# Attention of a decoder layer: products of raw x with the rms scale applied behind them, one scan per head, the first layer norm folded into the second, no transposes of h

## The reference

```
h      = x * rsqrt(mean(x*x) + 1e-6) * norm_w
q,k,v  = h Wq, h Wk, h Wv       (8 heads of 64); rope on q and k
f,g,o  = sigmoid(h Wbeta + b), sigmoid(h Wig + b), sigmoid(h Wog + b)   (one per head and token)
M_t    = M_{t-1} * f_t + g_t / 8 * k_t v_t^T ;  y_t = o_t * q_t M_t
x1     = layernorm(x + y Wout + bout)                 # first layer norm
r_t    = 0.9 r_{t-1} + ctx_t * ctx_t
x2     = layernorm(x1 + x1 * r)                       # second layer norm
out    = layernorm(x2 + FFN(x2)),  FFN: 8 experts, 512 -> 2048 -> 512, with its own norm in front
```

## Time and profile before

| | us |
|---|---|
| median of 3 runs | 1409.67 |
| lowest and highest of the runs | 1406.32, 1410.07 |
| the profiled execution, its own time | 1414.41 |
| span of the profiled execution | 1412.6 |
| PE busy in the span | 1332.6 (94%) |
| DVE busy | 816.3 (58%) |
| POOL busy | 637.2 (45%) |
| ACT busy | 470.9 (33%) |

### The profile page before, as it was taken

One profiled execution on the slowest core, in us unless ns is written; L12 is line 12 of the kernel. 1 busy time (PEld: TensorE's weight loads), 2 busy tenths in 40 slices (PEclk: granted clock), 3 DMA queues, 4 the chain that ended last, 5 costly groups with the idle time before them and its releaser, 6 DMA issues.

```text
span 1412.6 us, 17999 instructions
## 1 busy us (share of the span) xinstructions
PE 1332.6 (94%) x6458; PEld 1051.4 (74%) x6458; DVE 816.3 (58%) x1464; ACT 470.9 (33%) x675; POOL 637.2 (45%) x357
## 2 busy tenths in 40 slices
...
GB/s 227 60 60 76 60 48 57 74 74 74 60 74 60 30 74 74 60 46 112 75 231 60 63 200 44 212 94 48 200 60 197 108 32 214 60 178 128 21 129 30
DMA packets 63990, 133.66 MB, mean 95 GB/s; under 512 B 4800, under 2 KB 5440, under 8 KB 61888
## 3 DMA queue, kind: packets, MB, share of 16 engines
...
## 4 chain that ended last, share of the span: by engine, by line
PE 74%; DVE 18%; issue 5%; ACT 1%; DMA 1%; DVEq 0%; SPq 0%; POOL 0%; POOLq 0%; ACTq 0%
PE qk_ps L84 6%; PE qk_ps L86 6%; PE qk_ps L85 6%; PE v_ps L84 5%; PE v_ps L85 5%; PE v_ps L86 5%; DVE decays L855 4%; PE gate_ps L84 4%; PE gate_ps L86 4%; PE gate_ps L85 4%; PE y_ps L84 4%; DVE decays L854 4%; PE y_ps L85 3%; PE y_ps L86 3%; PE s_ps L84 3%
## 5 line engine op out<-in xcount | busy, mean ns | idle before, releaser
L695 POOL TENSOR_TENSOR rot<-rot 128x1024 f32<-128x1024 f32 x32 | 81.8, 2557 | 254.1 <-DVE rot L880 254.1
L1025 DVE CAST yT_hi<-gate_ps 128x512 fp32r<-128x512 f32 x62 | 42.9, 692 | 180.8 <-ACT gate_ps L630 180.8
L1025 DVE CAST yT_hi<-v_ps 128x512 fp32r<-128x512 f32 x62 | 42.9, 691 | 172.4 <-ACT v_ps L630 172.4
L84 PE MATMUL qk_ps<-wqkv_hi,hT 128*128 128x512 f32 x256 | 103.6, 405 | 2.4 <-DVE wqkv_lo L807 2.4
L630 ACT ACTIVATE gate_ps<-gate_ps,b_cols 128x512 f32<-128x512 f32 x64 | 42.2, 660 | 190.1 <-PE gate_ps L86 190.1
L85 PE MATMUL qk_ps<-wqkv_lo,hT 128*128 128x512 f32 x256 | 100.0, 391 | 0.0
L86 PE MATMUL qk_ps<-wqkv_hi,hT 128*128 128x512 f32 x256 | 99.6, 389 | 0.0
L769 POOL TENSOR_TENSOR wqkv_lo<-h_squares,wqkv_hi 128x2048 fp32r<-128x2048 f32 x15 | 69.3, 4623 | 66.9 <-ACT wqkv_hi L597 66.9
L733 POOL TENSOR_TENSOR rstd_b<-mean_var_b,ln_eps_b 128x4 f32<-128x4 f32 x15 | 3.0, 202 | 211.4 <-DVE mean_var_b L1013 211.4
L630 ACT ACTIVATE v_ps<-v_ps,b_cols 128x512 f32<-128x512 f32 x64 | 42.3, 661 | 157.2 <-PE v_ps L86 156.3
L855 DVE TENSOR_TENSOR_SCAN decays<-f_all,diag 128x128 f32<-128x128 f32 x128 | 89.0, 695 | 0.0
(11 more groups left out here) (267 smaller groups left out, 3784.3 us busy)
## 6 DMA issues: line engine op xcount, KB each, us to landing
...
```

The costliest lines, as they stand in the source:

```text
L84: eng.matmul(out, lhs_hi, rhs_hi, start=first, stop=False)
L695: pool.tensor_tensor(a, a, rot_b[j], ALU.add).then_inc(rot_done, 1)
L1025: dve.tensor_copy(high, up_ps[c % 2][:]).then_inc(hid_hi_done, 1)
```

## The change

The rms scale depends on the token alone, so it can be applied behind the products. The changed kernel therefore:

- loads x a second time, already transposed (`xT`, an input laid out by the host), and splits it on ACT (`x_high`) and POOL (`x_low`). `scale_h`, `turn_h`, `h_high` and `h_low` are gone, and with them 8 transposes on PE;
- puts the rms scale into the rope tables (`scale_rope` on ACT), into the gate of v (`token_gates`) and, for the gates, into a product with `rms_rows`, which reach all rows through a small round trip to DRAM (`spread_rms`);
- makes one scan of 384 elements per head of the two of 256 and 128, with a zero between the parts (`clear_f`), two DMAs for the two parts of `f_all`, one buffer of decays in place of two, and another order of scans;
- leaves the first layer norm out as a pass: `add_memory` subtracts its mean on the way, and since the second norm divides by its own deviation, the first deviation enters only through its epsilon (`norm_scale`, six small POOL instructions in place of two times two). The second normalisation moves from DVE to ACT (`scale_x2`);
- orders the bodies anew on PE, DVE, ACT and POOL.

The core of the diff (left out: allocation, waits renamed from h to xT, and where the expert stage's buffers lie):

```diff
-SCANS = {3: (0,), 4: (1, 2), 5: (3, 4, 5), 6: (6, 7)}
+SCANS = {3: (0, 1), 5: (2, 3, 4, 5), 7: (6, 7)}
...
+            def load_xT(b):
+
+                if b.n >= 1:
+                    sp.wait_ge(xT_lo_done, (b - 1).after(1, 1))
+                sp.dma_start(xT_raw[:], xT[b.index].rearrange("(k p) t -> p k t", p=P)).then_inc(xT_in, 16)
...
+            def spread_rms(b):
+
+                sp.wait_ge(rms_done, b.after(1, 1))
+                for j in range(NT):
+                    sp.dma_start(rms_dram[b.odd, j * P:(j + 1) * P].rearrange("(p a) -> p a", a=1), rms[:, b.odd, j:j + 1])\
+                        .then_inc(rms_stored, 16)
+                sp.wait_ge(rms_stored, b.after(32, 32))
+                sp.dma_start(rms_rows[:], rms_dram[b.odd].partition_broadcast(NG)).then_inc(rms_in, 16)
...
+                rows = f_dram[b.odd].rearrange("(h t) -> h t", h=NH)
+                sp.dma_start(f_all[:, :, P:DW], rows.partition_broadcast(P)).then_inc(f_in, 16)
+                sp.dma_start(f_all[:, :, 0:P], rows[:, P:L].partition_broadcast(P)).then_inc(f_in, 16)
...
+                if (b + 1).within(B):
+                    spread_rms(b + 1)
                 if (b + 2).within(B):
                     load_x(b + 2)
+                    load_xT(b + 2)
...
+            def x_high(b):
+
...
+                act.activation(xT_hi[b.odd], xT_raw[:], ACT.Copy).then_inc(xT_hi_done, 1)
+
+            def scale_rope(b):
...
+                for j in range(NT):
+                    act.activation(rope_x[:, j, :], rope_sb[:, j, :], ACT.Copy,
+                                   scale=rms[:, b.odd, j:j + 1]).then_inc(rope_scaled, 1)
...
+            def scale_x2(b):
+
+                act.wait_ge(shift_done, b.after(1, 1))
+                for j in range(NT):
+                    act.activation(res[:, j, :], res[:, j, :], ACT.Identity, bias=shift[:, j:j + 1],
+                                   scale=rstd[:, j:j + 1]).then_inc(x2_done, 1)
...
+                    if (b - 2).within(B) and b.n <= B and c == 0:
+                        scale_x2(b - 2)
...
                 if (b + 1).within(B):
-                    h_high(b + 1)
...
+                if b.n >= 0 and (b + 1).within(B):
+                    scale_rope(b + 1)
...
+                    if e.i is None and e.n == 0 and c == 1:
+                        scale_x2(Step(B - 1))
...
+            def x_low(b):
+                pool.wait_ge(xT_hi_done, b.after(1, 1))
+                pool.tensor_tensor(xT_lo[b.odd], xT_raw[:], xT_hi[b.odd].bitcast(F32), ALU.subtract).then_inc(xT_lo_done, 1)
...
+            def norm_scale(b):
+
+                pool.wait_ge(mean_done[1], b.after(NT, NT))
...
+                    pool.wait_ge(x2_done, (b - 1).after(NT, NT))
+                pool.tensor_tensor(shift[:], mean_var[0][:, :, 1], ln_eps[:], ALU.add).then_inc(eps_scaled, 1)
+                pool.wait_ge(eps_scaled, b.after(2, 1))
+                pool.tensor_tensor(shift[:], shift[:], ln_eps[:], ALU.mult).then_inc(eps_scaled, 1)
+                pool.wait_ge(eps_scaled, b.after(2, 2))
+                pool.tensor_tensor(rstd[:], mean_var[1][:, :, 1], shift[:], ALU.add).then_inc(var_eps, 1)
+                pool.wait_ge(var_eps, b.after(1, 1))
+                pool.tensor_tensor(rstd[:], rstd[:], minus_half[:], ALU.pow).then_inc(rstd_done, 1)
+                pool.tensor_tensor(shift[:], mean_var[1][:, :, 0], minus_one[:, 0:NT], ALU.mult).then_inc(minus_mean, 1)
+                pool.wait_ge(rstd_done, b.after(1, 1))
+                pool.wait_ge(minus_mean, b.after(1, 1))
+                pool.tensor_tensor(shift[:], shift[:], rstd[:], ALU.mult).then_inc(shift_done, 1)
...
+                    if b.n == -1:
+                        x_low(b + 1)
                     rms_scale(b + 1)
+                    if b.n >= 0:
+                        x_low(b + 1)
                 if (b - 2).within(B):
-                    norm_scale(b - 2, 1)
+                    norm_scale(b - 2)
                 if (b - 1).within(B):
                     context_low(b - 1)
                 if b.n == B:
                     split_w2(Step(0), 0)
                 if b.within(B):
                     rotate(b, 0)
+                if (b + 1).within(B):
+                    residual(b + 1)
+                if b.within(B):
                     rotate(b, 1)
                 if b.n == B - 1:
                     expert_scale(Step(0), 0)
-                if (b - 1).within(B):
-                    norm_scale(b - 1, 0)
-                if b.n == B - 1:
                     first_w1_low()
-                if (b + 1).within(B):
-                    residual(b + 1)
...
+                dve.tensor_tensor(gates_sum[:], gate_ps[0:NG, 0:L], gates_sum[:], ALU.add).then_inc(gates_added, 1)
+                dve.wait_ge(gates_added, b.after(1, 1))
+                dve.wait_ge(rms_in, b.after(16, 16))
+                dve.tensor_tensor(gates_sum[:], gates_sum[:], rms_rows[:], ALU.mult).then_inc(gates_summed, 1)
...
+                for j in range(NT):
+                    dve.tensor_scalar(g_tok[:, j, :], tok[:, j, NH:2 * NH], rms[:, b.odd, j:j + 1], float(DH) ** -0.5,
+                                      ALU.mult, ALU.mult).then_inc(gates_tok, 1)
...
+                dve.memset(f_all[:, :, P:P + 1], 0.0).then_inc(f_cleared, 1)
...
-                dve.tensor_tensor_scan(decays[:, b.odd, n, P:DW], f_all[:, n, :], diag[:, P:DW], 0.0, ALU.mult, ALU.add)
-                dve.tensor_tensor_scan(decays[:, b.odd, n, 0:P], f_all[:, n, P:L], diag[:, 0:P], 0.0, ALU.mult, ALU.add)\
-                    .then_inc(decay_done, 1)
+                dve.wait_ge(f_cleared, b.after(1, 1))
...
+                dve.tensor_tensor_scan(decays[:, n, :], f_all[:, n, :], diag[:], 0.0, ALU.mult, ALU.add).then_inc(decay_done, 1)
...
-            def normalize(b, n):
-                dve.wait_ge(rstd_done[n], b.after(1, 1))
-                for j in range(NT):
-                    dve.tensor_scalar(res[:, j, :], res[:, j, :], mean_var[n][:, j, 0:1], rstd[n][:, j:j + 1],
-                                      ALU.subtract, ALU.mult).then_inc((x1_done, x2_done)[n], 1)
...
-                    dve.tensor_tensor(res[:, j, :], c_sb[b.odd][:, j, :], res[:, j, :], ALU.mult).then_inc(u_done, 1)
+                    dve.scalar_tensor_tensor(out=res[:, j, :], in0=res[:, j, :], scalar=mean_var[0][:, j, 0:1],
+                                             in1=c_sb[b.odd][:, j, :], op0=ALU.subtract, op1=ALU.mult).then_inc(u_done, 1)
...
-                    if (b + 1).within(B) and n == 6:
-                        scale_h(b + 1)
                     if b.within(B) and n == 3:
                         rope_parts(b, 0)
+                        clear_f(b)
                     if b.within(B):
                         for m in SCANS.get(n, ()):
-                            if b.n != 0 or m < 6:
-                                scan(b, m)
+                            scan(b, m)
+                    if b.within(B) and n == 5:
+                        gate_v(b, 1)
...
-                            scan(b, 6)
-                            scan(b, 7)
-                if b.n == B + 1:
-                    normalize(b - 2, 1)
...
-                if (b + 1).within(B) and b.n != 0:
-                    h_low(b + 1)
+                if b.within(B):
+                    rope_parts(b, 1)
...
+                if (b + 1).within(B):
                     sum_gates(b + 1)
...
-                if (b + 1).within(B) and b.n >= 0:
-                    sum_gates(b + 1)
                 if b.n == B:
                     split_hidden(Step(0), 1)
-                if (b - 1).within(B):
-                    normalize(b - 1, 0)
...
-                if (b + 1).within(B):
-                    turn_h(b + 1)
                 if b.n == B:
                     cross_memory(b - 1)
+                if b.within(B):
+                    turn_qk(b, 0)
+                if (b + 1).within(B):
+                    gate_products(b + 1)
                 if (b - 1).within(B):
                     project_out(b - 1)
-                if (b + 1).within(B):
-                    gate_products(b + 1)
-                if b.within(B):
-                    turn_qk(b, 0)
```

245 lines of the change are left out of this document (110 added, 135 removed).

## The result

The changed kernel takes 1461.37 us (median of 4 runs, 1460.78 to 1461.87), the kernel before 1409.87 in the same comparison: ratio 1.0363, 95% interval 1.0332 to 1.0394. It is slower by 3.6%. The forecast was 1449, with 1438 to 1460 as its own range and 1422 to 1474 as the stated one; 1461 lies in the second and just outside the first. The profiled execution has a span of 1459.6 us.

The account below looks back on a forecast made before the run. PE was taken to bound the kernel, waiting on DVE's queue before the last values. 1412.6 + 51.4 (14 periods of 44.0 against 40.33) - 2.5 - 9.7 = 1451.8 us span, 1449 median; own range 1438 to 1460, stated 1422 to 1474.

Parts of the forecast that it names:

- The decisive step: POOL's `residual(b+1)` ahead of `rotate(b,1)` waits for DVE's residual sum; PE idles some 5.5 us in each of 14 bodies.
- The piece ahead of the last values: In each body, POOL's splits, scans and rope addition put the last values at +26.6 us, where it was +26.0.
- a sign that failed: PE's wait before the last values should stay near 2 us, with scans of 2 us and more beside POOL's rope addition.
- The worth of merging the scans: On DVE, one scan of 384 in place of 256 and 128 gives 0.02 us per head, nothing.
- The clock: Half clock on PE behind each 5.5 us wait costs 1.5 us a period, bounds 0 and 3.4.
- transition to the experts: ACT does DVE's last normalisation, so PE's 6.76 us wait and 3.0 us of half clock go: -9.7 us.
- Nothing of the change lies there: The expert stage, from 720 us on with PE busy 686 of 693 us, is untouched by the change.
- The start: First batches: PE's 4.28 us wait for the gates shrinks, -2.5 us (bounds +2 and -4.3); rms round trip costed at nothing.
- A: DVE and POOL's port: scans do not stand still for POOL, period 40.0 to 40.3 us, total 1395 us; chance 0.09.
- B: Batches: half clock costs 3.4 us instead of 1.5 and one cover fails, period 46.0, total 1477 us; chance 0.17.
- C: Batches: PE's wait is there but the clock stays up, period 42.5, total 1428 us; chance 0.12.
- D: Batches: `residual`'s wait is met early because output products come sooner; time within 0.3% (4 us) of before; chance 0.03.

Follow-up runs that it names:

- Experiments 1 and 2: The changed kernel with `residual` behind both rotations, 1357.2 us; the kernel before with only `residual(b+1)` moved between the two rotations, 1467.1 us.
- Experiment 7: The changed kernel with 22 idle identity products on PE ahead of the last transposes in each body from 1 on: 1441.3 us.
- Experiments 9 and 11: Two scans per head (256 and 128) again: in experiment 4, 1365.7 us; in the changed kernel as it is, 1479.65 us.
- experiment 4: The changed kernel with `residual` behind both rotations and `wg_raw` declared ahead of `wg_parts` again, as before the change: 1346.5 us.
- Experiment 8: experiment 4 with wq and wk split ahead of batch 0's gates, and these gates turned behind the first q and k products: 1341.5 us.

## Why the prediction was right, point by point

**The decisive step held.** It said that `residual` ahead of the last rotation closes a chain of output products, DVE's sum, `residual`, rope addition and gate, and that PE idles some 5.5 us in each of 14 bodies, some 75 in sum; the trace has 5.41 and 75.6. In the body shown, from the last values on: the output products' end 8.1 us later (said: 8.05), the rotation's gate done 6.8 behind that (said: 6.95), with each step as the rows said. Experiments 1 and 2 show that the step is the whole verdict: without it the kernel is 4% faster than before (0.9579).

**The piece ahead of the last values was over-sized.** The forecast had them at +26.6 at full clock. Experiment 7, which has the change's order at full clock, has them at +25.4 in the mean, so 1.2 too late, and this is nearly all by which its period of 41.24 falls short of the 42.5. Some 0.7 us of it is the end of `context_low`: put 4.2 us later than before, at +16.1, it came at +15.4 to +15.5 in most bodies. The rest is mostly the piece of first scan, rope addition and second scan behind it, 3.8 us where the sum has 4.2. That the first scan would wait for `context_low` and the second for the rope addition was right. The same piece explains a sign that failed: the wait before the last values should have stayed near 2 us and is 0.6, because DVE is done earlier and PE comes later (at +24.9 in experiment 7, where the forecast had +24.1). The starts of the cross memory lie 42.95 us apart, and the forecast's period was 44.0 (43.3 to 44.7), so the mechanism was right and the size just outside those bounds.

**The worth of merging the scans was put wrong.** "Merging them gives 0.02 per head, nothing" is about right for scans that run alone (3.49 us for four, 0.87 each, against 0.91 a pair) and wrong beside POOL, where each instruction waits for a turn. Experiments 9 and 11 put the merging at 1.2 us a batch. The time did not suffer from the error, since the sum was worked out with one scan per head and a turn for each; but it hid one of the edits from which the gain without the move comes. The price that the prediction took from the Trainium skill's page VectorE: DVE Perf Modes and set aside, section on the TRN2 errata, stands there for an fp32 `tensor_tensor` addition. Another page, DVE: opcode table, instruction layouts, handler registers and perf-mode slots, section Datapath and trigger behaviour, says that the scan runs at half throughput. The scans of 128, 256 and 384 elements took 0.39, 0.67 and 0.93 us, some 2.1 ns an element, which agrees with that: it is twice the 1.05 ns by which a plain `tensor_tensor` of 1024 elements (1.22 us) and one of 512 (0.68) differ per element in the changed kernel.

**The clock.** Said 1.5 us a batch, measured 1.7 (experiment 7). That activity releases the throttle and idle time brings it back is also what the Trainium skill says (TensorE: Matmul & The Clock Gate, the part on the HAM clock gate); the trace agrees, since the idle products alone brought the mean granted clock from 0.93 to 1.00.

**The sum of the span.**

| term | said | measured | from |
|---|---|---|---|
| period | 42.5 + 1.5 | 41.24 + 1.71 | experiment 7; 42.95 in all |
| 14 periods over 40.33 | +51.4 | +36.7 | |
| up to the first cross memory product | -2.5 | +8.0 | 96.5 against 88.5 |
| transition to the experts | -9.7 | -8.8 | see below |
| expert stage | 0 | +10.9 | placement |
| rest | 0 | +0.2 | |
| span | 1451.8 | 1459.6 | |

The last three come from the gelu operations. First and last start of one half of them, in the kernel before, after, and in experiment 4:

```profile
L630 ACT ACTIVATE v_ps<-v_ps,b_cols x64: 637/662/663, 685.2 to 1392.7; 128x512 f32<-128x512 f32 x64
```
```profile
L673 ACT ACTIVATE v_ps<-v_ps,b_cols x64: 629/662/663, 730.0 to 1439.6; 128x512 f32<-128x512 f32 x64
```
```profile
L673 ACT ACTIVATE v_ps<-v_ps,b_cols x64: 627/662/663, 624.9 to 1323.6; 128x512 f32<-128x512 f32 x64
```

They last 707.5, 709.6 and 698.7 us: with the buffers where they were, the change gains 8.8 here, because the 6.76 us wait of the earlier trace rows is down to 1.35, and the 3.0 us of half clock behind it are gone (the granted clock is 1.00 in the 5.9 us behind it):

```profile
748.47 0.50 PE L84 MATMUL s_ps<-w_hi,yT_hi 128*128 128x512 f32 x1 [1.35 <-DVE yT_lo L1063]
```

and the placement takes 10.9 back. "Nothing of the change lies there" failed for the expert stage: the prediction priced instructions and not the line that moved a declaration.

**The start failed.** The rms round trip was costed at nothing, "asked for at about +9, needed at about +31". In the batches that was right: asked for at +8.9, needed at +30.7 in the body shown, and DVE waited for it in none of the 14 periods. In the first batch it was asked for at 11.3 us and needed at 14.3, when DVE came to the gates' sum, and DVE waited 12.74 us; behind it in DVE's and ACT's queues stood the splits of wq and wk. The forecast's term for the start, -2.5 with bounds of +2 and -4.3, had no place for this. Experiment 8 shows that this order held back q by 13 us; that the first cross memory product gained only 1.6 from it shows that the start has other bounds too, and what share of the 8.0 us is whose stays open.

So 1461 is 12 above the forecast by errors that partly cancel: -14.7 for the batches, +10.5, +0.9 and +10.9 for the other stages, and +4.7 because the median lay at the profiled execution this time and not below it. That the total came within 1% is in part luck: the start, whose term had the other sign, and the placement, which had no term, made up for what the batches fell short. The verdict isn't luck, since it hangs on the chain that the trace shows.

Of the rivals, A (faster, 1395) wanted scans that run through beside POOL and last values at +24.1. The scans stood still, 3.98 us for two in the changed kernel, and the values came at +25.4 even at full clock. No rival and no sentence of the forecast had it that the other edits alone, without the move, would bring the period to 35.7. B had the half clock at 3.4; C had it at 0; both are refuted by experiment 7. D fell with PE's waits at the transposes.
